# A Perceiver block in fp32 on one core: first key weights by heads, first context half by quarters, constants earlier

## What is computed

```
x = x + xattn(layernorm(x), ctx, ctx)   # 32 query heads, 8 key/value heads of 128, rope, causal
x = x + attn(layernorm(x))              # 32 heads of 16, biases, causal
x = x + ffn(layernorm(x))               # base projection + 8 gated low-rank experts
```

## Time and profile before

| | us |
|---|---|
| median of 3 runs | 727.95 (727.66 to 728.04) |
| the profiled execution | 727.08 |
| its span, first to last instruction | 725.3 |
| TensorE busy in it | 707.9 (98%) |
| VectorE, ScalarE, GpSimd busy | 514.3, 373.2, 486.7 |

### The profile page before, as it was taken

How to read it: one execution, slowest core, us unless ns; L and a number is a source line. 1 busy time by engine, 2 the same in 40 slices (tenths; PEclk the granted TensorE clock), 3 DMA queues, 4 the chain that set the end, 5 groups by cost and what they waited for, 6 DMA issues and landing times.

```text
span 725.3 us, 12895 instructions
## 1 busy us (share of the span) xinstructions
PE 707.9 (98%) x4848; PEld 564.9 (78%) x4848; DVE 514.3 (71%) x811; ACT 373.2 (51%) x559; POOL 486.7 (67%) x366
## 2 busy tenths in 40 slices
PE   9999999799999999999999999998999999998997
PEld 7788887577778777778778778776777888887886
DVE  5756878857857767757757757757657888898735
ACT  5456664644643743653653564554236677664220
POOL 1898555777867867867867867846324799984630
PEclk9999999999999999999999999999999999999999
DMA  8554513131310311301311212200200100020003
GB/s 284 201 173 135 165 54 115 45 131 45 117 43 31 106 37 43 101 29 43 101 41 45 88 43 73 74 15 5 99 0 2 44 31 30 2 58 32 15 1 116
DMA packets 25561, 51.09 MB, mean 70 GB/s; under 512 B 2352, under 2 KB 10672, under 8 KB 25520
## 3 DMA queue, kind: packets, MB, share of 16 engines
q1 hardware_dynamic: 25520, 50.53, 20.8%
HBM read 40.04 MB, written 10.49 MB: 70 GB/s over the span
## 4 chain that ended last, share of the span: by engine, by line
PE 84%; DVE 7%; POOL 4%; ACT 2%; issue 1%; DMA 1%; SPq 0%; DVEq 0%; POOLq 0%
PE pj L1559 11%; PE sc L1651 10%; PE pj L1651 9%; PE pj L1750 8%; PE tp L1559 8%; PE pv L1545 5%; PE pv L1638 4%; PE tp L1651 3%; PE sc L1618 3%; PE pj L1920 3%; PE tp L1533 2%; PE sc L1800 2%; PE tp L1813 2%; PE pv L1824 2%; PE pj L1533 2%; PE tp L1625 2%
## 5 line engine op out<-in xcount | busy, mean ns | idle before, releaser
L493 POOL TENSOR_TENSOR sw<-sw,cst 128x512 f32<-128x512 f32 x72 | 101.0, 1403 | 37.9 <-ACT sw L673 37.7
L517 POOL TENSOR_TENSOR sm<-sm,mx 128x512 f32<-128x512 f32 x64 | 72.1, 1133 | 45.4 <-DVE mx L1197 26.9
L511 POOL TENSOR_TENSOR w<-raw,w 128x896 fp32r<-128x896 f32 x28 | 60.9, 2197 | 34.7 <-ACT w L658 34.7
L499 POOL TENSOR_TENSOR qr<-t,sw 128x512 f32<-128x512 f32 x54 | 73.4, 1359 | 7.8
L522 POOL TENSOR_TENSOR sm<-sm,rz 128x512 f32<-128x512 f32 x64 | 66.0, 1045 | 18.2 <-DVE rz L1212 18.2
L1559 PE MATMUL tp<-x,w 128*128 128x512 f32 x288 | 76.1, 400 | 1.4 <-ACT sw L673 1.4
L793 ACT ACTIVATE sm<-sm 128x512 f32<-128x512 f32 x64 | 40.4, 633 | 69.9 <-POOL sm L517 69.9
L1750 PE MATMUL pj<-xh,ws 128*128 128x512 f32 x192 | 64.3, 401 | 0.2 <-ACT kb L881 0.2
L1559 PEld LDWEIGHTS tp<-x,w 128*128 128x128 f32 x288 | 52.0, 188 | 11.8 <-ACT sw L673 1.7
L658 ACT ACTIVATE w<-raw 128x1792 fp32r<-128x1792 f32 x15 | 25.6, 1707 | 59.8 <-DVE raw L1089 59.8
L1216 DVE TENSOR_TENSOR cl<-pv,ch 128x1024 fp32r<-128x1024 f32 x32 | 39.1, 1222 | 22.7 <-ACT ch L801 22.7
(11 more groups left out here) (277 smaller groups left out, 1860.9 us busy)
## 6 DMA issues: line engine op xcount, KB each, us to landing
rawd<-in_w_d SPq DMA_DIRECT2D x16, 512.0 KB, 3.3
raw<-in_w_q SPq DMA_DIRECT2D x15, 512.0 KB, 3.3
kscr<-sm SPq DMA_DIRECT2D x16, 256.0 KB, 2.1
vscr<-sm SPq DMA_DIRECT2D x16, 256.0 KB, 2.6
kr<-kscr SPq DMA_DIRECT2D x8, 512.0 KB, 3.2
vv<-vscr SPq DMA_DIRECT2D x16, 256.0 KB, 2.6
raw<-in_w_k SPq DMA_DIRECT2D x4, 512.0 KB, 5.9
cT<-in_ctxT SPq DMA_DIRECT2D x4, 512.0 KB, 6.7
```

The costliest lines, as they stand in the source:

```text
L493: pool.tensor_tensor(bs(sw[par][:, :]), bs(sw[par][:, :]), rep(cst[:, C_SIN:C_SIN + S], HB), ALU.mult).then_inc(sin_done, 1)
L499: pool.tensor_tensor(o, bs(t1[par][:, :]), bs(sw[par][:, :]), ALU.add).then_inc(rope, 1)
L511: pool.tensor_tensor(w7[p][:, 1, c], raw[:, 1:8, :].rearrange("p n c -> p (n c)")[:, c], w7[p][:, 0, c].bitcast(F32), ALU.subtract).then_i ...
L517: pool.tensor_tensor(s3, s3, per_group(mx[:, c, :], 8), ALU.subtract).then_inc(subbed, 1)
```

## The change

Piece 0 is loaded in two transfers of 256 KB, one for each head, and its layout in DRAM and on chip is by heads. Between the two stand four transfers of 256 KB, one for each slice of the first context half. Piece 1 follows, then the constants, then the second context half in two transfers as before. ScalarE and VectorE split piece 0 head by head. t1 and swap of k0 now stand ahead of the second context half on their engines, those of k1 right behind it and ahead of the value piece 2; piece 3 is split after t1 and swap of k2. k0 goes slice by slice with high x high and low x high, then high x low; k1 and k2 take low x high last and wait only there for the low part. WARM_UP is 9 instead of 16.

```
-WARM_UP = 16
+WARM_UP = 9
...
-            load_piece(0)
-            load_ctx(0, 0)
-            load_ctx(0, 1)
+            sp.dma_start(raw2[0][:, 0:512], w_k[0][:, 0:512]).then_inc(s_wa, 16)
+            for k in range(KT):
+                load_ctx(k, k, 1, 0)
+            sp.dma_start(raw2[0][:, 512:1024], w_k[0][:, 512:1024]).then_inc(s_w[0], 16)
             load_piece(1)
-            load_ctx(1, 0)
-            load_ctx(1, 1)
             sp.dma_start(cst[:, :], consts).then_inc(s_const, 16)
+            for i in range(2):
+                load_ctx(KT + i, 2 * i, 2, 1)
             sp.wait_ge(plo_d, 1)
             load_piece(2)
...
-            piece_hi(0)
+            first_hi(0, s_wa, phi_a)
             ctx_hi(0, range(KT))
+            first_hi(1, s_w[0], phi)
             piece_hi(1)
+            swap_k(0)
             ctx_hi(1, range(KT))
+            swap_k(1)
             piece_hi(2)
-            for t, i in PHASE1:
+            for t, i in PHASE1[2:]:
...
                     swap_k(i)
-                    if i == 0:
+                    if i == 2:
                         piece_hi(3)
...
-            piece_lo(0)
+            first_lo(0, phi_a, plo_a)
             ctx_lo(0, range(KT))
+            first_lo(1, phi, plo_d)
+            dve.wait_ge(s_const, 16)
+            t1_k(0)
             ctx_lo(1, range(KT))
+            t1_k(1)
             piece_lo(2)
-            dve.wait_ge(s_const, 16)
-            for ki in range(NKT):
+            for ki in range(2, NKT):
                 t1_k(ki)
...
-                if ki in (0, 3, 8, 9, 11):
-                    piece_lo({0: 3, 3: 4, 8: 5, 9: 6, 11: 7}[ki])
+                if ki in (2, 3, 8, 9, 11):
+                    piece_lo({2: 3, 3: 4, 8: 5, 9: 6, 11: 7}[ki])
...
                 if ki == 0:
-                    order = [(k, part) for part in (0, 2, 1) for k in range(KT)]
+                    order = [(k, part) for k in range(KT) for part in (0, 2)] + [(k, 1) for k in range(KT)]
+                    pe.wait_ge(phi_a, 1)
+                elif ki < 3:
+                    order = [(k, part) for k in range(KT) for part in (0, 1)] + [(k, 2) for k in range(KT)]
+                    pe.wait_ge(phi, piece + 1)
+                else:
+                    low()
```

More of the change, by code:

```diff
@@ L121, in build @@
         wv1 = sb(p1, "wv1", [P, 2, KT, 512], F32R)
-        wk = [sb(p1, f"wk{i}", [P, 2, KT, 256], F32R) for i in range(2)]
+        wk = [sb(p1, f"wk{i}", [P, 2, 2 * KT, P], F32R) for i in range(2)]
         sb(p1, "gap_p1", [P, 3 * 1024])
@@ L206, in build @@
         s_x = [sem(f"s_x{i}") for i in range(4)]
-        s_ctx = [sem(f"s_ctx{i}") for i in range(4)]
+        s_ctx = [sem(f"s_ctx{i}") for i in range(KT + 2)]
+        s_wa, phi_a, plo_a = sem("s_wa"), sem("phi_a"), sem("plo_a")
         s_w = [sem(f"s_w{i}") for i in range(2)]
@@ L345, in load_x, with load_ctx @@
                 sp.dma_start(X[:, 2 * i:2 * i + 2, :], x[:, 2 * i:2 * i + 2, :]).then_inc(s_x[i], 16)
-            def load_ctx(half, i):
+            def load_ctx(s, k, n, half):
                 c = slice(half * HALF, (half + 1) * HALF)
-                sp.dma_start(cT[:, 2 * i:2 * i + 2, c], ctxT[:, 2 * i:2 * i + 2, c]).then_inc(s_ctx[2 * half + i], 16)
+                sp.dma_start(cT[:, k:k + n, c], ctxT[:, k:k + n, c]).then_inc(s_ctx[s], 16)
             def load_piece(j):
@@ L666, in ctx_hi @@
                 for k in ks:
-                    if k % 2 == 0:
-                        act.wait_ge(s_ctx[2 * half + k // 2], 16)
+                    if half == 0:
+                        act.wait_ge(s_ctx[k], 16)
+                    elif k % 2 == 0:
+                        act.wait_ge(s_ctx[KT + k // 2], 16)
                     hi(cT[:, k, c], cxh[:, k, c], chi)
+            def first_hi(i, loaded, s):
+                act.wait_ge(loaded, 16)
+                hi(raw2[0][:, i * 512:(i + 1) * 512].rearrange("p (k c) -> p k c", k=KT),
+                   wk[0][:, 0, i * KT:(i + 1) * KT, :], s)
             def swap(par, src):
@@ L1508, in k_tile, with low @@
                 g, h = K_TILES[ki]
-                piece, c = g // 2, slice(g % 2 * P, (g % 2 + 1) * P)
+                piece = g // 2
                 tok = slice(h * HALF, (h + 1) * HALF)
                 w = wk[piece % 2]
[L1512 to L1515, removed]
+                def low():
+                    if piece == 1:
+                        pe.wait_ge(plo_p, 1)
+                    elif ki:
+                        pe.wait_ge(plo_d, (1, None, 4, 5)[piece])
+                    else:
+                        pe.wait_ge(plo_a, 1)
                 if h == 1:
@@ L1522, in k_tile @@
                 if ki == 0:
-                    order = [(k, part) for part in (0, 2, 1) for k in range(KT)]
-                for n, (k, part) in enumerate(order):
[L1525 to L1531, removed]
+                    order = [(k, part) for k in range(KT) for part in (0, 2)] + [(k, 1) for k in range(KT)]
[3 more added lines that the diff above has]
+                    pe.wait_ge(phi, piece + 1)
+                else:
+                    low()
+                for n, (k, part) in enumerate(order):
+                    if ki == 0 and part < 2:
+                        pe.wait_ge((chi, clo)[part], k + 1)
+                    if ki < 3 and k == 0 and part == 2:
+                        low()
                     a, r = ((0, cxh), (0, cxl), (1, cxh))[part]
-                    last = pe.matmul(k_bank[ki % 4], w[:, a, k, c], r[:, k, tok],
+                    last = pe.matmul(k_bank[ki % 4], w[:, a, g % 2 * KT + k, :], r[:, k, tok],
                                      start=(n == 0), stop=(n == len(order) - 1))
@@ L2066 @@
     wd = rows(L0_xattn_Wd)
-    w_k = np.stack([wk[:, :, 256 * j:256 * j + 256].reshape(P, -1) for j in range(4)])
+    w_k = np.stack([wk[:, :, 256 * j:256 * j + 256].reshape(P, KT, 2, P).transpose(0, 2, 1, 3).reshape(P, -1)
+                    for j in range(4)])
     w_v = np.stack([wv[:, 2 * kp:2 * kp + 2, 512 * j:512 * j + 512].reshape(P, -1)
```

## The result

| | before | changed |
|---|---|---|
| median, us | 727.66 (11 executions) | 731.37 (11 executions) |
| ratio of executions | | 1.0046, 95% interval 1.0033 to 1.0059 |
| the profiled execution, its span | 727.08, 725.3 | 730.78, 728.9 |

One execution of the changed kernel took 2055.76 us, far from all others, and is left out of the ratio; the median of the other ten is 731.08. The change makes the kernel 0.46% slower, about 3.3 us. On the 727.95 us of the prediction that is 731.3, just past the upper end of its range (731.2), and the interval reaches down to 730.4. It is beyond the 0.2% that counted as a difference.

The account below looks back on a forecast made before the run. TensorE was taken to bound the kernel, so the start of value tile v0 decides: 1.0 us later, added to 727.95, gives 729.0 us (rounded to 728.95 below). The range was 727.2 to 731.2 us.

Parts of the forecast that it names:

- The gain at k1: Key tile 1 on TensorE would start at 8.6 us instead of 11.02, 2.4 us won.
- the curve of landed bytes: Landing times read off ScalarE's starts behind DMA waits in the old kernel, with no fixed cost per transfer.
- The chain to v0: From the fourth context low part to value tile 0, serial VectorE and ScalarE work of 8.5 us; v0 at about 26.15.
- The turns between VectorE and GpSimd: At the second half's context low parts, an exclusive SBUF lock makes them alternate; the low parts end at 17.3, not 14.3.
- My price of 3 us: Lock turns between VectorE and GpSimd would delay the end of the context low parts by about 3 us.
- The clock: Rival, chance 0.30: TensorE's clock falls in the 3.3 us idle before v0, costing 1.6 us more; 730.6 us.
- the likeliest case alone: Whole kernel: v0 later without a fall of the clock, 728.4 to 729.8 us; chance 0.38.
- Undisturbed: Rival, chance 0.15: context low parts run before GpSimd gets in, v0 at 22.8 to 24.3; 725.6 to 727.1 us.
- doesn't bite: Rival, chance 0.17: earlier landings or fewer turns leave v0 within 0.5 us of its old start; 727.5 to 728.4 us.
- nine warm-ups: Rival, no chance given: clock stays at 1.2 GHz through k0, k1 2.0 us later than forecast, covered by v0's gap.
- The cover downstream: After v0, about 4 us of cover for later piece loads, priced at nothing; the shift neither grows nor shrinks.

Follow-up runs that it names:

- the early split: The changed kernel with the high part of piece 2 ahead of swap 1 on ScalarE and that of piece 3 ahead of swap 2; 726.05 us, ratio 0.9973.
- GpSimd held: The changed kernel, but GpSimd begins the rope of k0 only when VectorE has finished the eight context low parts; 729.43 us, ratio 1.0015.

## Why the prediction came out as it did

*The gain at k1* was forecast as 2.4 us and was 1.5. The step that was mis-sized is the curve of landed bytes. ScalarE took up the second key half at 8.86 (forecast 7.65) and piece 1 at 10.14 (8.9); the constants landed at 10.53 (9.3). All of the 1.2 us was lost ahead of the second key half; from there the steps to piece 1 and to the constants are as forecast. In the ten profiles with the new loads, the changed kernel's among them, piece 1 was taken up between 9.57 and 10.52 us; in the four with the old loads at 8.91 to 9.86. The means are 10.05 and 9.25. I had read that a transfer has no fixed cost in the queue. About 1 us for three more transfers is what these profiles suggest; no run changed the number of transfers alone, and the landings vary by 0.95 us among kernels with the same loads. The fit of the Trainium skill's page "DMA: Bandwidth & Descriptors", section "Anatomy of one DMA — SWDGE (gpsimd) path", would give an estimated 6 us if its fixed parts were added up; it was made for transfers issued by GpSimd, and those here are issued by SP. The profiles show far less. (Up to the last context transfer there are ten transfers for six, not for seven as the prediction counts, since the constants moved ahead; its curve of bytes doesn't use that number.)

*The chain to v0* was right in kind and length: low part of context, t1, swap, piece 2, t1, swap, piece 3, 8.6 us (forecast 8.5 to 8.8). It began an even 1.0 us later (18.31 for 17.3), inherited from the landing of the constants. v0 came at 26.91, forecast 26.15. That v0 and not k1 decides is shown by the early split: with k1 at 9.72, 0.2 us later than in the changed kernel, v0 starts at 23.59.

*The turns between VectorE and GpSimd* came as forecast: low part 4 at 1.13 us (1.1), 5 and 6 at 3.48 together (3.8), the last at 0.60. With GpSimd held they took 2.93 in all. The Trainium skill's page "SBUF — State Buffer", section "SBUF: two separate sides", with its exclusive lock agrees with both runs. My price of 3 us was for the end of the low parts; at v0 it was 1.3, since the hold itself put GpSimd's next work into the chain: in that run the low part of piece 2 took 2.25 us.

*The clock* was a rival with a chance of 0.30, and it is what happened; the likeliest case alone (728.4 to 729.8) was missed. The step that failed is that chance. I argued from one gap in one profile, and that trace had four gaps of over 1 us: the clock stayed up behind the three others (1.42, 1.14 and 1.83 us). Behind the forecast were three times of the kernel before, within 0.4 us of each other. The eleven of the comparison, these three among them, spread over 4.6 us (724.73 to 729.35). In the last set the standard deviation of the kernel before is 1.36 us over 35 executions, and 0.51 over twelve when its two late gaps are filled: the spread is mostly these falls. With a third gap of 2.8 us, nine of ten executions of the changed kernel have at least one fall by their mean clock, and eight have two or more. The one in front of v0 cost 1.7 us in the profile; filling its gap took 2.0 us off by the ratios.

*Undisturbed, doesn't bite, nine warm-ups:* none of the three occurred. In the changed kernel's profile the 0.43 us spacing ended near 6.3 us, early in k0, so whether the gap would cover a slow k0 was not tested; the number of warm-ups makes no difference there (the run with sixteen has v0 at 26.85 for 26.91).

*The cover downstream* held: the delay at k6 (31.31 - 27.88, 3.4 us) is that of the span (3.6), nothing was absorbed and little added.

*Sum.* Forecast +1.0 us, or +2.6 with the clock. Measured in the profile +3.4: start of v0 1.75 (of it 0.75 by later landings), clock 1.68.

## What to carry to other kernels

An earlier start on the engine that bounds the kernel is worth only what reaches the first tile that waits for something else: list what that tile waits for, and count the chain through the other engines' hand-written orders, not the bytes. When two engines take turns on an exclusive resource, look at what the new order makes ready at the same time. And before trusting a difference under 1%, look where the bounding engine idles close to 2 us or more in one piece: filling such gaps with matmuls whose result nobody uses made the kernel before 0.3% faster and took the standard deviation of its times from 1.4 to 0.5 us, and two short gaps looked safer than one long (one run).

## What the runs showed of the hardware

- A gap on TensorE was followed by a stretch at the 1.2 GHz level in some executions and not in others. Behind the 2.8 us gap near 502 us seven of eleven profiles without a filling there have one; the gap of 1.83 us near 670 us has one in three of twelve; of the gaps in front of v0, 2.77 and 2.21 us had one, 2.82 and 1.95 us had none. Two gaps of 1.42 and 1.16 us between 128 and 140 us stand in all fourteen profiles, and none was followed by one. The stretches were 3.41 or 6.83 us long; one of 3.41 us cost 1.7 us at v0, and one more fall in an execution of the changed kernel went with 0.9 to 1.5 us.
- The first rise of the clock is as variable. In all profiles but one the matmuls were at full rate by 7.5 us; in the kernel before with nine warm-ups and two short idles after them, the 0.43 us spacing lasted to 13.75. The granted clock reads 1.00 in the windows of that stretch all the same, as it does for the slow warm-ups; only the spacing shows the level. The Trainium skill's page "TensorE: Matmul & The Clock Gate", section "Part 1: The HAM clock gate (the "warmup" mystery)", calls the number of slow matmuls at the start variable from run to run; the runs here agree.
- VectorE and GpSimd took turns, one operation each. In the profiles with swap 0 ahead of the second context half and GpSimd free to start, the four low parts took 4.2 to 5.15 us, with it held 2.92 and 2.93; in the old order, with GpSimd's rope later, 3.58 with the new loads and 4.00 to 4.07 with the old, where they meet GpSimd's split of piece 1.
